# Grouping the last products of a batch ahead of the next batch's first projections, in a two-layer adaLN transformer kernel

## What is computed

```
x = x + ga * causal_softmax_attention(h)      # 16 heads of 64, keys/values from a rank-128 latent
x = x + gb * low_rank_gelu_mlp(h)
x = x + ga * performer_attention_and_mlp(h)   # 16 heads of 16, prefix sums
x = x + gb * expert_mixture(h)                # below
```

```python
grouped = x.reshape(x.shape[:-2] + (-1, ne, d))
logits = jnp.einsum('...btd,des->...btes', grouped, controller)
perm = (logits == jnp.max(logits, axis=-3, keepdims=True)).astype(x.dtype)
sel = jnp.einsum('...btd,...btes->...besd', grouped, perm)
inner = jax.nn.relu(jnp.einsum('...besd,desf->...besf', sel, f1) + bias)
inter = jnp.einsum('...besf,esfd->...besd', inner, f2)
out = jnp.einsum('...besd,...btes->...btd', inter, perm)
```

## Time and profile before

| | |
|---|---|
| median of 3 runs | 1732.9 us (1732.89 to 1733.78) |
| the profiled execution | 1733.78 us |
| its span on the core | 1732.4 us |
| PE busy | 1662.5 us, 96% |
| DVE, ACT, POOL busy | 1227.6, 847.9, 865.8 us |

### The profile page before, as it was taken

How to read it: one execution, slowest core, us unless ns; L and a number is a source line. 1 busy time by engine, 2 the same in 40 slices (tenths; PEclk the granted TensorE clock), 3 DMA queues, 4 the chain that set the end, 5 groups by cost and what they waited for, 6 DMA issues and landing times.

```text
span 1732.4 us, 41066 instructions
## 1 busy us (share of the span) xinstructions
PE 1662.5 (96%) x16518; PEld 1133.2 (65%) x16518; DVE 1227.6 (71%) x2678; ACT 847.9 (49%) x1864; POOL 865.8 (50%) x1123
## 2 busy tenths in 40 slices
PE   8999999999999999999999999999999999999997
PEld 5566685767566667566856667756684666766666
DVE  4988957626689994762678887675367999676545
ACT  5666634233577762422357765432245777443233
POOL 2788853141188884232128888314113888740410
PEclk9999999999999999999999999999999999999999
DMA  6566572141566655032346655405045666620504
GB/s 188 125 150 149 139 182 87 27 73 37 163 147 138 149 140 167 1 61 38 87 134 153 146 139 135 146 2 93 5 113 133 146 151 142 155 102 2 98 0 124
DMA packets 143853, 189.11 MB, mean 109 GB/s; under 512 B 34512, under 2 KB 107696, under 8 KB 142640
## 3 DMA queue, kind: packets, MB, share of 16 engines
q1 hardware_dynamic: 125472, 179.14, 42.1%
q10 hardware_dynamic: 18192, 7.35, 1.9%
HBM read 88.32 MB, written 13.16 MB: 59 GB/s over the span
## 4 chain that ended last, share of the span: by engine, by line
PE 61%; DVE 15%; ACT 6%; POOL 5%; SPq 5%; DMA 4%; issue 3%; POOLq 0%; ACTq 0%; DVEq 0%
PE scores L470 13%; PE bank L681 8%; PE scores L661 7%; SPq L1011 5%; PE bank L470 5%; DVE prob L800 5%; POOL placed L864 4%; DMA placed<-prob 4%; ACT prob L916 3%; PE bank L708 3%; PE scores L1711 2%; PE bank L718 2%; PE scores L1773 2%; PE scores L441 2%; PE scores L1368 1%
## 5 line engine op out<-in xcount | busy, mean ns | idle before, releaser
L864 POOL COPY placed<-prob 32x768 f32<-32x768 f32 x448 | 367.8, 821 | 216.7 <-DVE prob L800 186.0
L301 POOL TENSOR_TENSOR rstd<-rstd,minus_half 128x2 f32<-128x2 f32 x96 | 69.7, 728 | 506.9 <-DVE rstd L300 504.8
L681 PEld LDWEIGHTS bank<-placed,v_t 128*64 128x64 f32 x4608 | 250.7, 137 | 74.9 <-issue 73.2
L681 PE MATMUL bank<-placed,v_t 128*64 128x128 f32 x4608 | 272.6, 274 | 10.9 <-DMA placed<-prob 9.3
L661 PE MATMUL scores<-k_t,q_t 64*128 64x512 f32 (+3 forms) x1536 | 274.0, 496 | 1.1 <-DVE neg_max L793 1.0
L800 DVE STREAM_TRANSPOSE prob<-prob 128x1536 f32<-128x1536 f32 x128 | 222.5, 1764 | 46.7 <-ACT prob L916 46.5
L793 DVE CUSTOM_DVE_ANT_0 mod_rows<-scores,hx 128x128 f32<-128x128 f32 (+7 forms) x256 | 190.7, 745 | 32.1 <-PE scores L661 32.1
L661 PEld LDWEIGHTS scores<-k_t,q_t 64*128 64x128 f32 x1536 | 130.1, 187 | 112.9 <-issue 92.1
L864 POOL COPY placed<-hx 32x768 f32<-32x768 f32 x224 | 184.1, 822 | 33.3 <-DVE hx L800 16.6
L916 ACT ACTIVATE prob<-mod_rows,neg_max 128x128 f32<-128x128 f32 (+2 forms) x192 | 137.6, 717 | 117.6 <-DVE neg_max L793 113.9
L793 DVE CUSTOM_DVE_ANT_0 x<-scores,hx 128x128 f32<-128x128 f32 (+7 forms) x256 | 192.7, 753 | 0.0
(11 more groups left out here) (252 smaller groups left out, 3111.4 us busy)
## 6 DMA issues: line engine op xcount, KB each, us to landing
placed<-prob SPq DMA_DIRECT2D x576, 96.0 KB, 2.5
f<-in_L_ffn_f SPq DMA_DIRECT2D x16, 2048.0 KB, 13.6
placed<-hx SPq DMA_DIRECT2D x288, 96.0 KB, 2.2
inverse_wide<-inverse_scratch SPq DMA_DIRECT2D x64, 256.0 KB, 4.3
slots_scratch<-high_rows SPq DMA_DIRECT2D x16, 512.0 KB, 6.6
inter<-slots_scratch SPq DMA_DIRECT2D x32, 256.0 KB, 4.7
mod_rows<-mod_scratch SPq DMA_DIRECT2D x32, 128.0 KB, 5.0
out<-x SPq DMA_DIRECT2D x16, 256.0 KB, 2.1
```

The source lines that it names most:

```text
L301: step = pool.do(lambda e, ts=ts: nc.gpsimd.tensor_tensor(rstd[:, ts], rstd[:, ts], minus_half[:, ts], op=ALU.pow), var, filled)
L681: last = nc.tensor.matmul(out_bank[rows_, at_:at_ + P], v_t[pair % 2][:, j, rows_], placed[m % 2][:, :, head, first_block(m, i) + j, :], s ...
L864: nc.gpsimd.tensor_copy(placed[m % 2][target * GROUP:(target + 1) * GROUP, source, :, :, :], prob[m % 3][source * GROUP:(source + 1) * GRO ...
```

## The change

Four things are changed.

1. `final_pair` takes its bank from the rotation, and all four pairs of every batch are emitted in that batch, after `slot_rows`. The next batch's `q0` and `q1` come after all of them and wait for the last readers of banks 6 and 7; `k0` to `v1` come after that and wait for the last readers of all banks and for the latent.
2. `k0` and `k1` of the first pair of heads are copied out by DVE (`first_job`), with a semaphore of their own, `job_read_dve`; ACT copies `q0`, `q1`, `v0`, `v1`. The numbers that others wait for follow (`act_job_number`).
3. `load_pair` for the next batch is issued by SP after the `write_slots` of both parts, and no longer before the first.
4. `load_batch` is appended to SP's lane at the start of `batch`; its place behind the stores and before `sp_pairs` is the same.

```diff
@@ batch, start
+        if b > 0:
+            sp.do(load_batch)
...
+        before_pairs = [r for r in banks.readers if r is not None]
+        before_queries = banks.readers[6:8] + [first_shift]
...
@@ pe_pairs
                 if m % ROUNDS_OF == 0:
-                    e.wait_ge(flow["job_read_act"], base["job_read_act"] + job_number(pair, "k1"))
+                    e.wait_ge(flow["job_read_act"], base["job_read_act"] + act_job_number(pair, "k1" if pair else "q1"))
+                    if pair == 0:
+                        e.wait_ge(flow["job_read_dve"], base["job_read_dve"] + 2)
...
                 if pair == 0 and kind == "v":
-                    e.wait_ge(flow["job_read_act"], base["job_read_act"] + job_number(0, JOBS[2 + half]))
+                    e.wait_ge(flow["job_read_dve"], base["job_read_dve"] + half + 1)
...
+            for j in JOBS[2:]:
+                job(0, j)
             for m in range(ROUNDS):
                 scores(m)
...
@@ dve_pairs
+            def first_job(j):
+                e.wait_ge(flow["job_done"], base["job_done"] + job_number(0, j))
+                nc.vector.tensor_copy(k_t[0][:, int(j[1]) * HW:(int(j[1]) + 1) * HW], bank_of(0, j)).then_inc(flow["job_read_dve"], 1)
...
+            first_job("k0")
+            first_job("k1")
             for m in range(ROUNDS):
...
@@ act_pairs
-            for j in JOBS:
+            for j in ("q0", "q1", "v0", "v1"):
                 job(0, j)
...
@@ the lanes around the first pair of heads
-        for j, first, last in ((None, 0, 1), (0, 1, 2), (1, 2, 4)):
-            if j is not None:
-                pe.do(lambda e, j=j: pe_pairs(e, ("first job", j)), banks.readers[6 + j], first_shift)
-            for pair in range(first, last) if b else ():
-                carry["final_pair"](2 * pair, banks)
-        if b:
-            sp.do(load_batch)
         sp.do(sp_pairs)
-        pe.do(lambda e: pe_pairs(e, ("keys and values", 0)), *banks.readers[0:2], *lat_done)
-        pe.do(pe_pairs, *banks.readers, *silu_late)
+        pe.do(lambda e: pe_pairs(e, ("queries", 0)), *before_queries)
+        pe.do(pe_pairs, *before_pairs, *lat_done)
...
@@ the end of the batch
-        if b + 1 < NB:
-            sp.do(lambda e: load_pair(e, 0, loaded["w0"]), done)
-            sp.do(lambda e: load_pair(e, 1, loaded["w1"]))
         for part_ in range(2):
             rows_product(part_)
+        if b + 1 < NB:
+            sp.do(lambda e: load_pair(e, 0, loaded["w0"]))
+            sp.do(lambda e: load_pair(e, 1, loaded["w1"]))
...
-        def final_pair(first, banks):
-
-            i = 2 + first // 2
-            ps, reader = all_banks[i], banks.readers[i]
+        def final_pair(first, *copies):
+
+            i, ps, reader = banks.take()
...
-        if b + 1 == NB:
-            for first in range(0, T, 2):
-                final_pair(first, banks)
+        for first in range(0, T, 2):
+            final_pair(first, *copies[first:first + 2])
```

More of the change, by code:

```diff
@@ L554, in batch @@
                      "normed": ROUNDS,
-                     "job_done": len(JOBS) * PAIRS, "job_read_act": len(JOBS) * PAIRS}
+                     "job_done": len(JOBS) * PAIRS, "job_read_dve": 2,
+                     "job_read_act": len(JOBS) * PAIRS - 2}
         base = {name: b * count for name, count in PER_BATCH.items()}
@@ L624, in job_number, with act_job_number @@
             return len(JOBS) * pair + JOBS.index(j) + 1
+        def act_job_number(pair, j):
+            return job_number(pair, j) - (2 if pair or j[0] == "v" else 0)
         FIRST_BANK = {"q0": score_tiles[1][:, 1, :], "q1": score_tiles[1][:, 2, :]}
@@ L633, in bank_read @@
             jobs = [(0, "v1" if out else "v0")] + [j for n in range(min(m, ROUNDS)) for j in jobs_of(n)]
-            return job_number(*[j for j in jobs if in_out_bank(*j) == out][-1])
+            return act_job_number(*[j for j in jobs if in_out_bank(*j) == out][-1])
         def bank_read_ahead_of(pair, j):
@@ L639, in bank_read_ahead_of @@
             jobs = [k for k in jobs if in_out_bank(*k) == in_out_bank(pair, j)]
-            return job_number(*jobs[jobs.index((pair, j)) - 1])
+            return act_job_number(*jobs[jobs.index((pair, j)) - 1])
         MOD_ROUND = 3
@@ L669, in values @@
                 if m % ROUNDS_OF == 0:
-                    e.wait_ge(flow["job_read_act"], base["job_read_act"] + job_number(pair, "v1"))
+                    e.wait_ge(flow["job_read_act"], base["job_read_act"] + act_job_number(pair, "v1"))
                 e.wait_ge(flow["job_read_act"], base["job_read_act"] + bank_read(m + 2 + (m + 2 < FILLING), True))
@@ L731, in mod_products @@
             def mod_products():
[L732 removed]
+                e.wait_ge(flow["job_read_act"], act_job_number(*jobs_of(0)[1]))
                 e.wait_ge(loaded["wmod0"], 16)
@@ L757, in pe_pairs @@
                 kind, m = only
[L758 to L761, removed]
+                if kind == "queries":
+                    return [job(0, j) for j in JOBS[:2]]
                 return values(m)
+            for j in JOBS[2:]:
+                job(0, j)
             for m in range(ROUNDS):
@@ L1024, in batch @@
         PAIRS_DONE = [(flow[k], (b + 1) * PER_BATCH[k])
-                      for k in ("job_read_act", "normed", "exp_done", "kept")]
-        silu_late = []
+                      for k in ("job_read_dve", "job_read_act", "normed", "exp_done", "kept")]
         if b == 0:
-            silu_late.append(act.do(lambda e: nc.scalar.activation(silu[:, 1, :, :], cond[:, 1, :, :], ACT.Silu),
-                                    (loaded["cond1"], COND)))
+            before_pairs.append(act.do(lambda e: nc.scalar.activation(silu[:, 1, :, :], cond[:, 1, :, :], ACT.Silu),
+                                       (loaded["cond1"], COND)))
             act.do(lambda e: nc.scalar.activation(spare_column[:, :], minus_half[:, 0:1], ACT.Exp))
@@ L1897, in combine @@
                 return last
-            done = pe.do(combine, reader, *copies[first:first + 2], block_done[first], block_done[first + 1],
+            done = pe.do(combine, reader, *copies, block_done[first], block_done[first + 1],
                          (landed[first // 2], 2 * 16 * (b + 1)))
@@ L1918, in batch @@
                 prologue.latent(1)
-        if b + 1 == NB:
-            for first in range(0, T, 2):
-                final_pair(first, banks)
+        for first in range(0, T, 2):
+            final_pair(first, *copies[first:first + 2])
         return {"readers": banks.readers, "at": banks.at, "prior_x": prior_x, "h_read": [sel_product[-1], turned_read],
-                "lat_done": prologue.done if prologue else None, "final_pair": final_pair}
+                "lat_done": prologue.done if prologue else None}
     carry = {"readers": [None] * 8, "at": -1, "prior_x": [None] * 3, "h_read": [], "lat_done": None}
```

2 lines of the change are left out of this document (1 added, 1 removed).

## The result

The changed kernel took 1744.08 us at the median of 5 runs (1742.87 to 1747.28), the kernel before 1733.78 (1732.89 to 1737.98): 10.3 us more, a ratio of 1.0058 with a 95% interval of 1.0041 to 1.0076. The direction was forecast, the size not: 4.9 us were predicted, and 1744.08 lies above the range. Of the 6.3 us by which it misses 1737.8, 0.9 lie in the base: the forecast started from 1732.9, the median of three runs. In later comparisons the kernel before had medians of 1735.1 to 1735.7, with single runs from 1730.6 to 1738.8. Its profiled execution, on which the prediction rests, is one of the quick ones.

What follows compares the result with a forecast made beforehand. PE, busy 96% of the span, was taken as the bound. Three boundaries at 1.5 us plus four batches at 0.1 us for DVE's key copies gave +4.9 us on 1732.9: 1737.8 us, range 1735.2 to 1742.8.

Steps and rivals of the forecast that it cites:

- its wait for bank 2: At each batch boundary, PE's 0.35 us idle before pair 0's `combine`, which the new banks were to remove.
- the queries wait for DVE: At each boundary `q0` waits about 0.9 us until DVE's gate multiplication empties banks 6 and 7.
- the delay is passed on: After each boundary, the scores' 1.5 us delay was taken to reach the batch's end in full.
- the fourth landing: At each boundary, the fourth pair's scratch reads land 9.75 us after the reads start, 451.35 at the first boundary.
- R: Start of the scratch reads at a boundary, forecast to move from 442.9 to 441.6 at the first.
- that fits, so 0: On SP, six loads needing 3.4 to 4.6 us fit the 4.9 us before the reads, costing 0.
- The clock: Rival: PE's clock falls in the boundary gaps, up to 3.7 us a boundary; 1741.5 us, chance 0.08.
- the landing is later than computed: Rival: scratch reads at the boundaries land later, held by SP or the loads; 1741.5 us, chance 0.16.
- The rule on ring order: DMA engines consume descriptors in ring order, so loads issued last leave the scratch writes undelayed; mixing could cost 2.6 us.
- Not slower: absorbed: Rival: the value products' wait for `placed` swallows the 1.5 us boundary delay; 1732.9 us, chance 0.12.

Runs made afterwards that it cites:

- e4: The changed kernel with the `w_ring` loads issued by SP after the eight scratch reads: 1742.75 us, ratio 1.0053 to the kernel before.
- e2: The kernel before with only the `w_ring` loads moved behind the scratch writes: 1735.81 us, ratio 1.0000.
- e24: The changed kernel with loads issued after the reads and pairs in banks 4, 5, 2, 3: 1739.75 us, ratio 1.0029 to the kernel before.
- r1: The changed kernel run once more, unaltered: 1744.27 us, ratio 1.0055 to the kernel before.
- e6: The changed kernel with its pairs in banks 4, 5, 2, 3, so the first queries wait for no pair: 1742.19 us, ratio 1.0046 to the kernel before.
- d2: The changed kernel with two more 256 KB reads ahead of the eight scratch reads: 1750.84 us, ratio 1.0085 to the kernel before.
- e8: The kernel before with its four pairs in banks 4, 5, 2, 3 in place of 2, 3, 4, 5: 1733.95 us, ratio 0.9991.
- e12: The kernel before with both queries ahead of all four pairs, and banks 4, 5, 2, 3: 1734.52 us, ratio 0.9989.
- e5: The kernel before with `k0` and `k1` of the first pair copied out by DVE: 1737.55 us, ratio 1.0016.
- e1: The changed kernel with the `w_ring` loads put back ahead of the scratch writes: 1743.19 us, ratio 1.0048 to the kernel before.

## Why the prediction was wrong

**What held.** The cost is idle time of PE, and it arose at the boundaries. The pairs stand in a row, the first starts without its wait for bank 2 (but for the 0.21 us that it waits for DMA at the first boundary), the queries wait for DVE (0.95, 0.85 and 0.85 us computed as 0.9), part 2 costs 0.14 a boundary (0.1), and the delay is passed on. With the landing that it assumed, the sum is right: e4's first boundary has it, and its stretch is 33.05 against 32.95.

**The step that failed: the fourth landing, R + 9.75 with R = 441.6, "that fits, so 0".** In the frame of the table it put the last landing at 23.55 for every boundary. In the six boundaries of the changed kernel's two profiles it was at 24.6 to 27.1, 25.5 on average. That is 1.9 us later, and behind the landing everything is fixed (9.3 us to the scores, unless PE's clock falls), so three boundaries cost 5.8 us more. It has two parts.

- *R.* The reads started at 14.7 to 16.0, 15.2 on average, and not at 13.8: 1.4 us. Of this 0.8 us is SP's time: the reads started up to 1.9 us after the writes had landed. I had priced the six loads at 3.4 to 4.6 us, within SP's 4.9, from rows where the DMA engines had room (and the 3.4 was read wrongly: the loads took 2.8 us there, and then SP waited for the copies that the writes need); behind the writes they took 5.6 to 6.8. The other 0.6 us is the writes themselves. They landed at 14.1 to 14.2 at five of the six boundaries, and in e2, against 13.7 to 13.8 with no load behind them (e4 and e24, first and second boundary); at the sixth they landed at 15.4. So part 3, meant in the sum to bring R forward by 1.27 us at two boundaries, put it back. Undone (e4), R is 13.8 at two of three boundaries. At the third, and in e24 again, the writes themselves took 11.6 and 12.3 us to land; that has nothing to do with the loads.
- *From R to the landing.* 9.75 us came from one reading, the end of batch 3. It fits its own trace: there the four places have 9.5 to 9.8 us from the first read to the last landing. (By the matmuls that it released the reading is 0.14 us long, and the steps behind it are 0.2 us shorter than I had them.) But in the changed kernel it is 9.75 to 11.1 us, 10.2 on average: 0.5 us. One execution couldn't show this spread.

A part of the late R could have been read before the run. I let the third boundary pass as a repetition of the first, but its writes took longer to land:

```profile
1282.86 5.66 SPq L1818 DMA_DIRECT2D slots_scratch<-high_rows  x4
1294.00 5.00 SPq L1859 DMA_DIRECT2D inter<-slots_scratch  x8
```

These are 11.1 us from the writes to the reads, not the 10.3 of the other three places. The last landing came at 24.8 and 24.9 at the first and third boundary of this trace, and part 3 could take back only what the loads had held the writes up, 1.3 and 0.7 us.

**The clock.** This rival came true in part: at one of six boundaries it cost 1.7 us (r1). At the first boundary of the changed kernel it fell too, behind 2.71 us of idle time:

```profile
448.00:450.00 2.00, 1.27 (x13) 0.68 (x16) 0.00 (x0) 0.00 (x0) 0.00 (x0) 0.50 1.00 290
450.00:452.00 2.00, 1.99 (x24) 0.66 (x16) 1.25 (x2) 0.00 (x0) 0.00 (x0) 0.64 0.17 51
```

but there the second and third pair bore it, while the last read was in flight anyway. Over all the grouped kernels seven idle times at the boundaries were 2.0 to 2.7 us long. Behind five of them the clock fell to its lower level (2.71 in the changed kernel, 2.03 in r1, 2.15 in e6, 2.05 and 2.41 in d2), behind two it didn't (2.21 in e4, 1.99 in e24), and behind no shorter one. It cost 1.7 us in r1, 2.8 in e6 and 0.1 or less in the other three. The gap of 0.9 us, for which I had given the rival its chance, never did it by itself. The page that I cited, "TensorE: Matmul & The Clock Gate" of the Trainium skill, section "HAM oscillation — how this bites in real kernels", describes waits for DMA between bursts of matmuls that leave the clock at its lower level. It is borne out in kind only: its waits are longer than any gap at these boundaries, so for gaps of 0.9 us it gave no reason to move the sum towards this rival.

**The sum again, with measured terms.** Three stretches of 25.5 + 9.3 = 34.8 us, plus on average 0.9 for the clock in a profile, are 10.7 us more than the kernel before's three (94.6 in all). The two profiles of the changed kernel have 10.5 and 11.0. The medians differ by 10.3 in the first comparison and 8.6 in the other, and both profiled executions (1745.32 and 1748.72) lie above their medians. The rest of batches 1 to 3, from the first scores to the next `rows_product`, took 393.7 to 395.6 us in the kernel before and its variants (394.5 on average) and 393.8 to 396.1 in the changed kernel and its variants (394.8). So what the change costs outside the boundaries is small, about 1 us in all if anything, and the figure of any one execution is scatter.

**The rival "the landing is later than computed"** was thus the case that occurred, with a chance of 0.16 and priced at 1741.5, at worst 1743.9. Its reasons were R and the loads; the spread from the first read to the last landing wasn't among them, so that its worst price comes near the measured time is in part luck. The rule on ring order that I cited beside part 3 ("DMA: Bandwidth & Descriptors", section "Queues, rings and completion order", of the Trainium skill) was not the point. At the first boundary the writes landed at 14.2 with the loads behind them and at 13.7 without (e4), 0.4 us later and not the 2.6 that mixing could have cost, so on the bytes the trace nearly agrees. The larger part was SP's time, which the rule doesn't touch. **"Not slower: absorbed"** is refuted: the waits for `placed` are 9.1 us against 9.3.

What stays open is why a last read now and then lands 1 to 2 us late, with an issue of 2.7 us once. It happens with and without loads, and in both orders: from the first read to the last landing it took 11.2 us once in e8 and 10.4 once in e12. On average it is 9.9 us over the boundaries of the kernel before, e2, e5, e8 and e12 and 10.2 over those of the changed kernel, r1, e1, e4, e6 and e24, so that the grouping itself slows the reads by a few tenths isn't excluded. The cause wasn't tried.

## What to carry to other kernels

Independent work between a chain of transfers and its consumers covers not just the mean of their landing but its spread, and a sum made from one execution doesn't see that. Compare the same transfers at every place in the trace, and in more than one execution, before a sum rests on one landing, and place the covering work ahead of the consumers. Price DMA issues by a row in which the DMA engines are as full as they will be, and a copy given to another engine by what that engine's queue holds at that moment.

## What the runs showed of the hardware

An issue on SP took longer while earlier transfers filled the DMA engines: at the first boundary of the changed kernel 128 KB took 1.99 us to issue behind 2 MB of writes, with the DMA engines busy for 0.96 of the time, and 0.44 us five microseconds later, when they were busy for 0.07. So moving small loads behind large writes held up SP, by up to 1.9 us beyond the landing of the writes, while the loads' bytes made the writes land only 0.4 us later. Reads issued in order didn't always land in order: at the first boundary of the changed kernel the fourth landed at 23.7 and the fifth at 23.05 us. The Trainium skill says in "DMA: Bandwidth & Descriptors", section "Two DMAs through the same engine are not ordered", that nothing orders DMAs across the engines, and this trace agrees.
